# Recomputing every head's exponentials in the second attention pass, with ScalarE copying finished pairs out of PSUM

## The reference, cut to what matters

```python
dots = jnp.einsum('bhnd,bhmd->bhnm', q, k) * temp
dots = fq_floor(dots)                    # int8 with one scale for the whole tensor
attn = jax.nn.softmax(dots, axis=-1)
attn = fq_floor(attn)                    # the scale needs the largest weight of all heads
out = jnp.einsum('bhnm,bhmd->bhnd', attn, v)
```

## Time and profile before

| | us |
|---|---|
| time, median of 3 runs (2971.46 to 2976.84) | 2971.98 |
| the profiled execution's own time | 2968.33 |
| its span, first to last instruction | 2966.5 |
| score stage, roughly | 714 to 1094 of the span |
| weighting stage, first exponential to the last maximum | 1105.37 to 1458.42 |

### The profile page before, as it was taken

How to read it: one execution, slowest core, us unless ns; L and a number is a source line. 1 busy time by engine, 2 the same in 40 slices (tenths; PEclk the granted TensorE clock), 3 DMA queues, 4 the chain that set the end, 5 groups by cost and what they waited for, 6 DMA issues and landing times.

```text
span 2966.5 us, 44556 instructions
## 1 busy us (share of the span) xinstructions
PE 2619.6 (88%) x13128; PEld 1004.7 (34%) x13176; DVE 2410.9 (81%) x4227; ACT 1411.6 (48%) x2424; POOL 159.3 (5%) x147
## 2 busy tenths in 40 slices
PE   7999989995888857777769799999999999999997
PEld 4544432221111114444335322222223444444443
DVE  5988859999999979999888589889888865555554
ACT  3330033332999989999622145555556322221211
POOL 0000023330000000000000000111100000000000
PEclk9999999995555559999989899999999999999999
DMA  8563212223766656655315544334455520000000
GB/s 320 183 215 143 99 64 99 99 92 128 268 244 237 251 208 223 218 211 209 132 43 166 162 92 110 104 100 111 112 160 184 204 86 29 29 29 29 28 29 29
DMA packets 203518, 406.35 MB, mean 137 GB/s; under 512 B 33144, under 2 KB 119160, under 8 KB 182768
## 3 DMA queue, kind: packets, MB, share of 16 engines
q1 hardware_dynamic: 199072, 387.92, 38.6%
q10 hardware_dynamic: 4304, 16.78, 1.4%
HBM read 232.16 MB, written 172.46 MB: 136 GB/s over the span
## 4 chain that ended last, share of the span: by engine, by line
PE 50%; issue 25%; DVE 13%; ACT 6%; DMA 4%; DVEq 0%; SPq 0%; ACTq 0%; POOLq 0%; POOL 0%
PE bank L1117 8%; PE bank L1283 7%; PE bank L1272 7%; DVE stats L1588 5%; PE bank L1073 4%; PE bank L1081 4%; PE bank L1057 4%; PE bank L1171 3%; ACT arena L1430 3%; ACT arena L1419 3%; DMA arena<-dq_scr 2%; DMA arena<-e_scr 1%; PE bank L891 1%; PE bank L898 1%; PE bank L1089 1%
## 5 line engine op out<-in xcount | busy, mean ns | idle before, releaser
L1588 DVE TENSOR_REDUCE stats<-bank 128x1024 f32 (+1 forms) x352 | 406.5, 1219 | 45.3 <-PE bank L955 27.0
L1397 ACT ACTIVATE arena<-arena 128x512 bf16<-128x512 int8 (+1 forms) x512 | 360.9, 706 | 60.5 <-DVE arena L1825 57.1
L978 PE MATMUL bank<-arena 64*128 64x512 bf16 x512 | 306.4, 605 | 67.5 <-DVE arena L1836 25.2
L1836 DVE CUSTOM_DVE_ANT_0 arena<-bank,arena,fac 128x512 int8<-128x512 f32 x512 | 355.1, 756 | 12.9 <-ACT arena L1397 8.7
L2016 DVE TENSOR_REDUCE arena<-bank 128x2 f32<-128x1024 f32 x256 | 312.5, 1223 | 50.1 <-PE bank L1073 34.4
L1494 ACT ACTIVATE arena<-bank 128x1024 f32<-128x1024 f32 x256 | 248.0, 1022 | 187.9 <-PE bank L1089 187.9
L1564 ACT ACTIVATE arena<-bank,bf_s,fac 128x512 f32<-128x512 f32 x128 | 99.5, 778 | 434.1 <-PE bank L1275 434.1
L1377 ACT ACTIVATE arena<-bank,floor_c,fac 128x1024 int8<-128x1024 f32 x96 | 115.5, 1204 | 343.5 <-PE bank L918 292.9
L1117 PE MATMUL bank<-arena 128*32 128x512 f32 x2048 | 270.0, 604 | 0.0
L918 PE MATMUL bank<-arena 128*128 128x512 bf16 x989 | 241.9, 384 | 14.6 <-DMA arena<-hq_scr 7.4
L1283 PE MATMUL bank<-arena 128*128 128x512 f16 x1024 | 245.6, 379 | 7.6 <-DVE arena L2213 7.1
(11 more groups left out here) (216 smaller groups left out, 3507.2 us busy)
## 6 DMA issues: line engine op xcount, KB each, us to landing
e_scr<-arena SPq DMA_DIRECT2D x40, 1024.0 KB, 4.1
arena<-e_scr SPq DMA_DIRECT2D x40, 1024.0 KB, 4.8
dq_scr<-arena SPq DMA_DIRECT2D x128, 256.0 KB, 2.3
arena<-half_scr SPq DMA_DIRECT2D x256, 128.0 KB, 2.8
qkv_scr<-arena SPq DMA_DIRECT2D x8, 3072.0 KB, 9.7
arena<-dq_scr SPq DMA_DIRECT2D x88, 256.0 KB, 3.0
arena<-in_x SPq DMA_DIRECT2D x16, 1024.0 KB, 8.2
half_scr<-arena SPq DMA_DIRECT2D x32, 512.0 KB, 4.0
```

The source lines that it names most:

```text
L978: return mm(dst, qE[r, h // 2, P * t:P * t + P], kE[r, h // 2, :], start=True, stop=True)
L1397: last = A(dst[:, t, :], dq8[:, h % 4, t, :], ACT.Exp, bias=negm_b[:, par, c:c + 1], scale=exp_scale, accum_out=sum_b[:, par, c:c + 1])
L1588: return V.tensor_reduce(dst, src, ax, ALU.max, apply_absolute_value=True)
L1836: V.tensor_tensor_reduce(dq8[:, s, t, :], bank[:, 4 * (h % 2) + t, :], floor_row, fac[:, C_DOTS:C_DOTS + 1], -3.0e38, ALU.add, ALU.max, ac ...
```

## The change

No exponentials are kept any more: `e_scr`, `eS`, `eL`, `store_e`, `load_e` and `next_e` go, and all 16 heads of a batch take the way of the redone ones. DVE loses `pair_out`, which goes to ACT's list: the copy of pair p is written behind the exponentials of head 2p+5 (on DVE it stood behind the weights of head 2p+3). `pair_peak` stays on DVE, one pair later than before. In the first load group SP now issues `load_v` ahead of `load_dq`. The table of row factors `rq_g` goes. The semaphores `kept0` and `kept1`, which several stages shared, are split by stage, and the arena is 4 KB a partition smaller.

```diff
             def sums(b, par):
                 for h in range(H):
                     act.wait_ge(S("sum_done"), b * H + 4 + h - 1)
                     act.wait_ge(S("negm_ready"), b * H + h + 1)
-                    dst = e_dump[:, NT * (h % 2):NT * (h % 2) + NT]
-                    if h in KEPT_E:
-                        j = KEPT_E.index(h)
-                        dst = eS[:, (par + j) % 2]
-                        act.wait_ge(S(f"kept{(par + j) % 2}"), 2 * 8 * NB + NK * 8 * b - NK * 8 * par + 16 * ((NK * par + j) // 2) + 16)
...
+            def pair_out(b, p):
+                act.wait_ge(S("pvG_mm"), b * H + 16 + 2 * p + 2)
+                A(pair_of_o(b * PAIRS + p), bank[:, 4 + p % 4, :], ACT.Copy).then_inc(S("oG_evac"), 1)
+
             def weigh(b, par):
                 for s in range(H):
...
-                    if s in KEPT_ACT:
-                        act.wait_ge(S("eL_in"), (b * NK + KEPT_E.index(s) + 1) * 16)
-                        if not (is_batch(b, 0) and s < 2):
-                            act.wait_ge(S("aG_turned"), b * H + s - 1)
-                        for t in range(NT):
-                            c = NT * s + t
-                            A(aG[:, s % 2, t, :], eL[:, t, :], ACT.Identity, bias=round_c[:, :],
-                              scale=rq_g[:, par, c:c + 1]).then_inc(S("aX_done"), 1)
-                        continue
...
+                        A(eG[:, s % 2, t, :], dqG[:, s % 4, t, :], ACT.Exp, bias=negm_g[:, par, c:c + 1],
                           scale=exp_scale).then_inc(S("eG_done"), 1)
+                    if s % 2 and not (is_batch(b, 0) and s < 5):
+                        pair_out(b, (s - 5) // 2)
             through(act, weigh)
+            pair_out(NB, -2)
+            pair_out(NB, -1)
             barrier(act, 7)
...
-            def pair_out(b, p):
-                dve.wait_ge(S("pvG_mm"), b * H + 16 + 2 * p + 2)
-                V.tensor_copy(pair_of_o(b * PAIRS + p), bank[:, 4 + p % 4, :]).then_inc(S("oG_evac"), 1)
-
...
-                    if s % 2 and not (is_batch(b, 0) and s < 3):
-                        pair_out(b, (s - 3) // 2)
-                    if s % 2 == 0 and not (is_batch(b, 0) and s < 4):
-                        pair_peak(b, (s - 4) // 2)
+                    if s % 2 == 0 and not (is_batch(b, 0) and s < 6):
+                        pair_peak(b, (s - 6) // 2)
...
-            load_dq(0, 0)
-            load_e(0, 0)
-            for h in (2, 3):
+            load_v(0, 0)
+            for h in range(4):
                 load_dq(0, h)
-            load_v(0, 0)
```

More of the change, by code:

```diff
@@ L49 @@
 ENGINES = 5
[L50 to L56, removed]
 STAGES = (3, 5, 6, 7, 8, 9, 13)
@@ L200, in decoder @@
             "qkv_red": 4,
+            "hq_stored0": 16,
+            "hq_stored1": 16,
             "qkv_conv": 4,
-            "kept0": 16,
-            "kept1": 16,
+            "qkv_stored0": 16,
+            "qkv_stored1": 16,
             "qkv_mm": DUOS,
@@ L459, in store_hq @@
                 sp.wait_ge(S("hq_ready"), b + 1)
-                sp.dma_start(hq_scr[b], hqC[:, b % 2]).then_inc(S(f"kept{b % 2}"), 16)
+                sp.dma_start(hq_scr[b], hqC[:, b % 2]).then_inc(S(f"hq_stored{b % 2}"), 16)
             for b in range(NB):
@@ L512, in store_qkv @@
                 sp.wait_ge(S("qkv_conv"), b * DUOS + 4 + DUOS)
-                sp.dma_start(at4(qkv_scr, b), qkvD[:, par]).then_inc(S(f"kept{par}"), 16)
+                sp.dma_start(at4(qkv_scr, b), qkvD[:, par]).then_inc(S(f"qkv_stored{par}"), 16)
             ahead(sp, load_hq, store_qkv)
-            sp.wait_ge(S("kept0"), 16 + 2 * 8 * NB)
-            sp.wait_ge(S("kept1"), 16 + 2 * 8 * NB)
+            sp.wait_ge(S("qkv_stored0"), 16 + 16 * NB // 2)
+            sp.wait_ge(S("qkv_stored1"), 16 + 16 * NB // 2)
             barrier(sp, 5)
@@ L534, in _ @@
                 load_pair(0, p)
[L535 to L542, removed]
+            with sp.Fori(0, NB - 1) as b:
                 for p in range(PAIRS):
@@ L545, in pairs_dma @@
                     store_dq(b, 2 * p + 1)
[L546 to L553, removed]
+                    load_pair(b + 1, p)
+            for h in range(H):
+                store_dq(NB - 1, h)
             for s in range(4):
@@ L559, in load_dq @@
             def load_dq(b, h):
[L561 to L567, removed]
+                sp.wait_ge(S("eG_done"), b * (H * NT) + 4 * h + 4)
+                hold(sp)
                 src = dq_scr[b * H + h] if isinstance(b, int) else dq_scr[bass.ds(b * H + h, 1)].rearrange("a p t j -> p (a t) j")
                 sp.dma_start(dqG[:, h % 4], src).then_inc(S(f"dqG_in{h % 4}"), 16)
[L571 to L587, removed]
             def load_v(b, par):
@@ L607, in heads_dma @@
                     if h < H - 4:
-                        if h + 4 in REDONE:
-                            load_dq(b, h + 4)
-                    elif more and h + 4 - H in REDONE:
+                        load_dq(b, h + 4)
+                    elif more:
                         load_dq(b + 1, h + 4 - H)
-                    for j, kept in enumerate(KEPT_E):
-                        if h == kept + (0 if kept in KEPT_ACT else 1):
-                            next_e(b, j)
             through(sp, heads_dma)
@@ L824, in widen @@
                     if d == 0:
-                        pool.wait_ge(S(f"kept{par}"), 8 * NB + b * 8 + 16 - 8 * par)
+                        pool.wait_ge(S(f"qkv_stored{par}"), b * 8 + 16 - 8 * par)
                     pool.wait_ge(S("qkv_evac"), b * DUOS + 2 + d + 1)
@@ L1389, in sums @@
                     act.wait_ge(S("negm_ready"), b * H + h + 1)
[L1390 to L1394 removed]
                     for t in range(NT):
                         c = NT * h + t
[L1397 removed]
+                        last = A(e_dump[:, NT * (h % 2) + t, :], dq8[:, h % 4, t, :], ACT.Exp, bias=negm_b[:, par, c:c + 1],
                                  scale=exp_scale, accum_out=sum_b[:, par, c:c + 1])
@@ L1757, in quantise_h @@
                 dve.wait_ge(S("h8_done"), b + 1)
-                dve.wait_ge(S(f"kept{par}"), b * 8 + 16 - 8 * par)
+                dve.wait_ge(S(f"hq_stored{par}"), b * 8 + 16 - 8 * par)
                 V.tensor_copy(hqC[:, par].rearrange("p a b -> p (a b)"), h8C).then_inc(S("hq_ready"), 1)
```

53 lines of the change are left out of this document (12 added, 41 removed).

## The result

The changed kernel takes 2961.94 us (median of 20 runs, 2959.13 to 2965.63), the kernel before 2971.28 (20 runs on the same chip): a ratio of 0.997, 95% interval 0.9964 to 0.9976. Its profiled execution took 2962.11.

What follows compares the result with a forecast made beforehand. ACT was taken to set the pace in both the score and weighting stages. Terms -2.3 + 2.9 - 1.0 - 1.0 = -1.4 on 2968.3 gave 2966.9; with 3.7 for the median, 2970.6, say 2971 us; range 2963 to 2982.

Steps and rivals of the forecast that it cites:

- part 5: Score stage: stores and buffer waits go, ACT's waits at loop jumps may shrink; between 0 and -7.6, taken -1.0 us.
- rival C: Score stage gives all its waits back, 7.6 us instead of 1.0, to 2964 us; chance 0.12.
- ACT's stream: Weighting stage: scalings and their waits go, copies come at 0.49 us each; 345.7 to 343.4 us, term -2.3 us.
- Rival A: Weighting stage: a copy on ACT steps at 0.71 us, adding 13.4 us, to 2984 us; chance 0.12.
- DVE: Weighting stage: DVE rises from 40.8 to 42.1 us a batch but stays below ACT; nothing on the sum.
- Start of the stage: Weighting stage: values issued before levels move the first exponential from 1105.37 to about 1108.3; term +2.9 us.
- End: Weighting stage, last exponential to last maximum: 7.4 us becomes 6.4; term -1.0 us.
- B: Weighting stage: head 6's levels come late, ACT waits about 1 us in each of seven batches, to 2978; chance 0.06.
- D: Weighting stage: PE's clock halved from 1.00, making the stage slower by tens of microseconds; chance 0.02.

Runs made afterwards that it cites:

- run 1: Kernel before with each 1 MB store of kept exponentials cut to 32 KB, another tensor loaded in their place: 2965.41 us against 2971.05, ratio 0.9981.
- run 3: Also called more_waits: changed kernel with five more long-satisfied waits a batch on ACT in the score stage; 2963.44 us against 2971.05, ratio 0.9977.
- run 5: Two kernels: changed kernel with the old score stage, either head 13's store or the other four cut to 32 KB; 2965.59 and 2965.47 us against 2971.6.
- run 6: Changed kernel with the pair copies back on DVE: 2990.89 us against 2973.34, ratio 1.0056.
- run 9: Changed kernel with the first levels loaded ahead of the values and one pair copy in eight on DVE: 2959.95 us against 2973.34, ratio 0.9954.
- run 8: Changed kernel with the first levels issued ahead of the 1 MB of values: 2960.2 us against 2971.05, ratio 0.9962.
- stores_back: Changed kernel with the old score stage put back: f32 exponentials, buffers, waits and 1 MB stores that nothing reads; 2972.16 us against 2971.05, ratio 1.0003.

## Why the prediction was wrong

The step that failed is part 5, "Score stage": -1.0 taken, -6.9 measured. Its bounds (nothing to -7.6) held the value, though they leave out a wait of 0.7 us that the earlier trace rows puts down to ACT itself (with it the waits sum to 8.3), and its mechanism had been named, in the part and in rival C; the choice within the bounds was wrong, and C was given 0.12. The reason given for the low value was that no wait names a transfer. It is no reason: the rows can't name an instruction transfer, they say "issue", or the engine's own last instruction, or the other engine that was held up first. What spoke for C lay in the rows: the waits stood only where loops jump back, in a stretch with a DMA share of 0.64, and the argument against it, that "DVE's jump shows in ACT's waits too, and its code stays as long", took the length of the code for the price. It is the store that is in flight ahead of the jump (runs 1, 3 and 5).

Point by point:
- **ACT's stream:** right. A step of 0.48 for a copy where 0.49 was taken, batches of 43.0 where 43.1 was, no wait but one of 0.98 us for `dq_scr` at 1204.06 in the whole stream: 343.9 us against 343.4 predicted. Rival A is out. The budget that the Trainium skill gives ("ScalarE: Activation LUTs", "Rules for kernel authors") is for an instruction whose bias is a pointer operand, and the pair copy has none; the prediction left this condition out. Taken as the step of this copy the budget gives some 0.73 us (an estimate from that page), and the trace does not agree: 0.48 for 512 elements. The Trainium skill's rule in the same section, VectorE and not ScalarE for simple operations such as adding and multiplying, does not carry over to the copies of this stage: with them on VectorE (run 6) it was 27 us longer.
- **DVE:** right. It stays just below ACT and is hidden; with eight copies on top it bounds the stage (run 6), with one it does not (run 9).
- **Start of the stage:** right, +2.7 for +2.9, and run 8 shows the cause, the order of the first two loads. The first exponential was foretold at 1108 less what the score stage gave back; 1108.3 - 6.4 is 1101.9, and it started at 1101.76.
- **End:** -0.6 for -1.0. The chain behind the last exponential is as listed; it took 6.8 us where I had put down 6.4, and which handover took the difference is open.
- **Rivals B and D:** neither happened. One wait of 0.98 us stands where B would have had seven, and the clock stayed at 1.00 and 0.50.

With -6.9 and the other terms as predicted the sum is -7.3, and 2970.6 becomes 2964.7: within the range, and still 2.8 above the measured 2961.94. What that is made of is open. Part is that the sum went on top of a median from three runs (2971.98, where 20 runs later gave 2971.28). The rest sits in scatter of stages that no edit touches: between its first and its last transposed score, cross-attention took 549.0 us in the profiled execution of before, 548.9 in the changed kernel and 553.9 in stores_back, with the same instructions there.

Left open too: the trace shows the instruction packets but not for which engine each is, nor on which of the 16 DMA engines it stood behind a store. That a packet belongs to a jump is inferred from its constant distance to the instruction behind the jump.

## What to carry to other kernels

Where an engine idles only at the point where its loop jumps back, look at what SP issued in the 3 to 6 us before: one 1 MB store there cost 0.6 to 1.4 us at a jump of ACT here, and 1.4 to 1.8 us at a jump of DVE. Moving, shrinking or dropping that one store gave back what no wait in the profile blames on it. And when work is traded between two engines that are both near full, add up start-to-start steps for both: either half of this trade alone made the stage 16.6 or 25.5 us longer, both together left it as it was.

## What the runs showed of the hardware

- An instruction transfer can come late behind a data store, and then the engine whose loop jumps back waits. The wait at the jump was 0.6 to 1.4 us on ACT with a 1 MB store issued 5.4 to 5.9 us ahead, and nothing that a row shows with a small store there or none; on DVE it was 3.2 us with a store issued 3.4 us ahead and 1.4 to 1.8 without. With no 1 MB store in the stage the stream was as short with 45 or 42 instruction packets as with 27 (362.2, 362.5 and 362.3 us).
- The length of an instruction can grow while its step does not. In the changed kernel's weighting stage the pair copies read 0.57 us at 1116 and 0.70 at 1445, and the exponentials 762 ns on average (706 before); in more_waits single exponentials reached 948 ns. The distance from one to the next stayed 0.61 us throughout, so a sum of lengths would have found a slowdown of 8% that wasn't there.
